# The second stage of a four-layer convolution: four x2 buffers, small products as scalar_tensor_tensor, later statistics products, and layer three's image scaled on two engines

## The reference

```python
def _gn(v, G=8, eps=1e-5):
    g = v.reshape(B_, G, C_ // G, H_, W_)
    m = jnp.mean(g, axis=(2, 3, 4), keepdims=True)
    s = jnp.var(g, axis=(2, 3, 4), keepdims=True)
    return ((g - m) / jnp.sqrt(s + eps)).reshape(v.shape)
...
    x = x + _L0_conv_ref(_gn(x), 5)          # five Newton-Schulz steps on each 128x128 plane
    x = x + _L1_conv_ref(_gn(x), L1_conv_weight_int8, L1_conv_scale_weight, L1_conv_bias)  # 8-bit input, 3x3
    x = x + _L2_conv_ref(_gn(x), L2_conv_filter_w)   # a diagonal filter of 5 taps
    x = x + _L3_conv_ref(_gn(x), L3_conv_weight)     # a 3x3 circular convolution (written with FFTs)
```

## Time and profile before

| | us |
|---|---|
| Median of three runs | 3712.34 |
| Lowest and highest of the three | 3697.12, 3731.15 |
| The profiled execution's own time | 3719.76 |
| Its span on the core | 3717.7 |

### The profile page before, as it was taken

How to read it: one execution, slowest core, us unless ns; L and a number is a source line. 1 busy time by engine, 2 the same in 40 slices (tenths; PEclk the granted TensorE clock), 3 DMA queues, 4 the chain that set the end, 5 groups by cost and what they waited for, 6 DMA issues and landing times. The chain is left out here.

```text
span 3717.7 us, 137014 instructions
## 1 busy us (share of the span) xinstructions
PE 3436.3 (92%) x58321; PEld 2903.0 (78%) x58321; DVE 2935.7 (79%) x6205; ACT 2514.6 (68%) x4686; POOL 2737.8 (74%) x3415
## 2 busy tenths in 40 slices
PE   7999999999999999999999994788888888888888
PEld 7999999999999999999999993344545455545445
DVE  5888888888888888888888885677777777777874
ACT  6766677777777767767777763676666666766763
POOL 6888888888888888888888874566666666656662
PEclk9999999999999999999999996899999999999998
DMA  2212112122211211212212212566666666666663
GB/s 67 69 58 58 61 56 68 61 60 64 69 59 58 69 58 58 69 58 58 69 58 58 69 42 73 118 159 153 144 167 145 147 166 147 165 143 144 157 145 87
DMA packets 317726, 347.23 MB, mean 93 GB/s; under 512 B 21568, under 2 KB 284224, under 8 KB 300736
## 3 DMA queue, kind: packets, MB, share of 16 engines
q1 hardware_dynamic: 317120, 338.47, 34.9%
HBM read 135.09 MB, written 134.22 MB: 72 GB/s over the span
## 5 line engine op out<-in xcount | busy, mean ns | idle before, releaser
L1462 PE MATMUL bank<-xn,wt 64*32 64x512 bf16 (+1 forms) x18432 | 969.6, 396 | 60.9 <-issue 33.8
L1462 PE MATMUL bank<-xn,wth 64*32 64x512 f16 (+1 forms) x6144 | 949.4, 396 | 9.5 <-issue 9.4
L1235 POOL TENSOR_TENSOR xn<-F,xn 128x512 f16<-128x512 f32 x512 | 539.3, 1092 | 349.1 <-ACT xn L1292 349.1
L487 ACT ACTIVATE P<-bank 128x512 f32<-128x512 f32 x1024 | 606.0, 607 | 266.0 <-PE bank L1010 155.0
L1462 PEld LDWEIGHTS bank<-xn,wt 64*32 64x32 bf16 (+1 forms) x18432 | 453.9, 95 | 201.8 <-issue 85.5
L1462 PE MATMUL bank<-xk,wt 64*32 64x512 f16 x9216 | 535.2, 384 | 66.3 <-issue 47.5
L1462 PE MATMUL bank<-xk,wth 64*32 64x512 f16 x3072 | 524.0, 384 | 17.3 <-issue 17.1
L1462 PEld LDWEIGHTS bank<-xn,wth 64*32 64x32 f16 (+1 forms) x6144 | 407.7, 95 | 151.8 <-issue 25.9
L1349 DVE SCALAR_TENSOR_TENSOR x<-bank,wu,x 128x512 f32<-128x512 f32 x512 | 367.6, 743 | 165.0 <-PE bank L1462 163.8
L1245 POOL TENSOR_TENSOR x<-x,X 128x512 f32<-128x512 f32 x256 | 322.3, 1277 | 207.8 <-ACT x L1306 207.4
L1306 ACT ACTIVATE x<-bank,bst,sws 128x512 f32<-128x512 f32 x256 | 189.3, 776 | 386.2 <-PE bank L1462 197.0
(11 more groups left out here) (147 smaller groups left out, 8501.3 us busy)
## 6 DMA issues: line engine op xcount, KB each, us to landing
xk<-xn SPq DMA_DIRECT2D x1024, 65.9 KB, 2.6
X<-in_x SPq DMA_DIRECT2D x64, 1024.0 KB, 4.8
x_scratch<-X SPq DMA_DIRECT2D x64, 1024.0 KB, 6.0
X<-x_scratch SPq DMA_DIRECT2D x64, 1024.0 KB, 6.3
out<-x SPq DMA_DIRECT2D x64, 1024.0 KB, 4.4
wf<-in_w SPq DMA_DIRECT2D x2, 192.0 KB, 6.9
wf<-in_w SPq DMA_DIRECT2D x1, 320.0 KB, 7.2
whf<-in_w1h SPq DMA_DIRECT2D x6, 1.0 KB, 5.8
```

The source lines that it names most:

```text
L487: nc.scalar.activation(into[:, 4 * q:4 * q + 4, :], banks[q][:, :].rearrange("p (m w) -> p m w", m=4), ACT.Copy).then_inc(sb, 1)
L1235: ins = nc.gpsimd.tensor_tensor(padded(xn[l][n % 2], 1)[:, a + 1:a + 5, L:L + H], F[l][:, a:a + 4, :], padded(xn[l][n % 2], 0)[:, a + 1:a ...
L1462: ins = nc.tensor.matmul(bank[cols_, :], w, v, start=(half == i == 0), stop=(half == 1 and i == length[l] - 1))
```

## The change

1. `x2` has four buffers in place of three, so the first `raise_` of an image waits for the image four before.
2. A helper `product` writes the small products of `deviations` (one) and `normalise` (three) as scalar_tensor_tensor with the scalar 1.0, in place of tensor_tensor.
3. TensorE issues `mean` after the first piece of layer three instead of before it, and `var` after the second instead of the first. VectorE takes the first `chunk_stats` of the new image ahead of `deviations`, and `normalise` after the third piece's statistics instead of the second's.
4. ScalarE issues `quotients` ahead of `root`.
5. For layer three, ScalarE writes the f16 upper half straight from `x3` (`upper3`), and VectorE writes `F3` from `x3` (`scale3`) right behind `normalise`. GpSimd's `lower(3, ...)` waits for both. Layer two keeps its two ScalarE passes.

```diff
-            THIRD = 3
-            xs = [None, x1s] + [[sb(f"x{l}_{n}", [H, NJ, H]) for n in range(k)] for l, k in ((2, THIRD), (3, THIRD))]
+            THIRD, X2 = 3, 4
+            xs = [None, x1s] + [[sb(f"x{l}_{n}", [H, NJ, H]) for n in range(k)] for l, k in ((2, X2), (3, THIRD))]
...
                         pool.wait_ge(high[l], n + 1)
+                        if l == 3:
+                            pool.wait_ge(scaled_f[3], n + 1)
...
+                    def upper3(n, b):
+
+                        act.wait_ge(scale_set, b + 1)
+                        need(act, normed[3], n)
+                        nc.scalar.activation(padded(xn[3][n % 2], 0)[:, 1:NJ + 1, L:L + H], xs_of(3, n)[:, :, :],
+                                             ACT.Identity, scale=cols["r"][:, 1:2],
+                                             bias=cols["nb"][:, 1:2]).then_inc(high[3], 1)
...
-                            need(act, evac[2], BPI * (n - 2))
+                            need(act, evac[2], BPI * (n - X2 + 1))
...
+                        if there(s + 1):
+                            quotients(s + 1)
                         if pair(s):
                             root(s - 1)
-                        if there(s + 1):
-                            quotients(s + 1)
                         if there(mid):
-                            upper(3, mid, s - 1)
+                            upper3(mid, s - 1)
...
+                    def product(out_, a, b):
+                        return nc.vector.scalar_tensor_tensor(out=out_, in0=a, scalar=1.0, in1=b, op0=ALU.mult, op1=ALU.mult)
...
-                        link.done(nc.vector.tensor_tensor(dev[:, :, :], dev[:, :, :], dev[:, :, :], ALU.mult))
+                        link.done(product(dev[:, :, :], dev[:, :, :], dev[:, :, :]))
...
+                    def scale3(n, b):
+
+                        dve.wait_ge(scale_set, b + 1)
+                        need(dve, normed[3], n)
+                        nc.vector.tensor_scalar(F[3][:, :, :], xs_of(3, n)[:, :, :], cols["m"][:, 1:2], cols["r"][:, 1:2],
+                                                ALU.subtract, ALU.mult).then_inc(scaled_f[3], 1)
...
                             whole_stats(s - 1)
-                            deviations(s - 1)
                         for u in range(BPI):
                             if there(s):
                                 chunk_stats(2, s, u)
-                            if u == 1 and pair(s):
+                            if u == 0 and pair(s):
+                                deviations(s - 1)
+                            if u == 2 and pair(s):
                                 normalise(s - 1)
+                                if there(mid):
+                                    scale3(mid, s - 1)
...
-                            mean(s - 1)
                         for u in range(BPI):
                             if there(three):
                                 piece(3, three, u)
                             if u == 0 and pair(s):
+                                mean(s - 1)
+                            if u == 1 and pair(s):
+                                if there(s):
+                                    finish(1, s, 0)
                                 var(s - 1)
```

More of the change, by code:

```diff
@@ L1387, in normalise @@
                         link.wait()
-                        link.done(nc.vector.tensor_tensor(c["rb"][:, :], c["ra"][:, :], c["ra"][:, :], ALU.mult))
+                        link.done(product(c["rb"][:, :], c["ra"][:, :], c["ra"][:, :]))
                         link.wait()
-                        link.done(nc.vector.tensor_tensor(c["rb"][:, :], c["rb"][:, :], c["ve"][:, :], ALU.mult))
+                        link.done(product(c["rb"][:, :], c["rb"][:, :], c["ve"][:, :]))
                         link.wait()
@@ L1393, in normalise @@
                         link.wait()
-                        link.done(nc.vector.tensor_tensor(c["r"][:, :], c["ra"][:, :], c["rb"][:, :], ALU.mult))
+                        link.done(product(c["r"][:, :], c["ra"][:, :], c["rb"][:, :]))
                         link.wait()
```

## The result

The changed kernel takes 3703.18 us in the median of 19 runs (3692.5 to 3717.32) against 3713.58 for the kernel before in 19 runs (3697.12 to 3731.15). The ratio is 0.9969 with a 95% interval of 0.9954 to 0.9983: 10 us faster, where I had forecast 36. The profiled execution took 3717.3 us, span 3715.1, the slowest of its runs; in this pair the traces differ by less than the medians do, so I read them for which waits moved and not for the last microseconds.

What follows compares the result with a forecast made beforehand. VectorE's chain was taken to bound the 16 short steps, which gain nothing; the 41 long ones gain 1.04 + 0.3 - 0.4 on TensorE, less 0.1. Mean 0.60 over about 60 steps gives 36 us, so 3676 us, range 3625 to 3728.

Steps and rivals of the forecast that it cites:

- `mean` one piece later: TensorE's wait for VectorE's sums at `mean`, 1.04 us a step, goes because the moved piece covers 2.1 us.
- `var`: TensorE waits at `var` for late sums of squares: +0.4 us a step, between 0 and 1.3.
- The clock: Half-clock stretches on TensorE behind `mean` go with its idle time: -0.3 us a step, between nothing and 0.43.
- Small products: On VectorE, scalar_tensor_tensor still waits for GpSimd's adds, so the exchange of operation itself is worth 0.
- The one row on which this stood: L1376 on VectorE, a scalar_tensor_tensor: median 177 ns, but 1.28 us once, at 3281.06, when an add began just before.
- Four `x2` buffers: The fourth buffer, with `quotients` ahead of `root`, gives 0; ScalarE's 174.8 us of waiting are mostly time it had to spend.
- `scale3` and the collision: VectorE's chain grows by 1.21 us for `scale3` and 1.09 for one collision of `clamp` with GpSimd's `lower(3)`.
- The upper bound of 2.2 us for `scale3`: On VectorE, `scale3` would take 2.2 us at one column per ns, as the statistics were said to have it.
- Short and long steps: 16 steps under 20 us, bound by VectorE's chain, gain nothing; 41 long ones, mean 22.1, gain 0.84 us each.
- the sign of being wrong that I had written down: Wrong if VectorE idles before `whole_stats` and steps stay at 21 us, or if products are short beside a running add.
- Layer three's upper half in one pass: ScalarE loses a 1.91 us pass; `lower(3)`, layer two and transfers into `xk` start about 1.9 earlier, without a gain term.
- an exchange of waits: Rival: all of `mean`'s wait returns at `var` and the next `mean`; within 15 us either way, 3712; chance 0.17.

Runs made afterwards that it cites:

- small store: The changed kernel with only the first of sixteen rows of each output tile stored, 64 KB an image in place of 1 MB: 3631.65 us, ratio 0.9766.

## Why the prediction was wrong

Against the forecast, point by point; per-step numbers are the totals of 2400 to 3600 us over 56 steps.

*`mean` one piece later.* Right: 1.04 forecast, 58.3 - 2.0 = 56.3 us, 1.0 a step. The kernel without `scale3`, that is the new order with the free parts alone, gained 1.6%, and the old order beside `scale3` lost some 50 us against the new one.

*`var`.* Right: 0.4 forecast, 22.0 / 56 = 0.39.

*The clock.* I took 0.3. In 2410 to 3550 us the windows of 1 us show 17 half-clock stretches before and 14 after, and 36 us lost before, 24 after, so 0.2. The size is near; the reason that I gave is wrong. I had put 14 of the stretches down to the wait at `mean` because they begin close to a `mean`. Of the 17 of before, 7 have a wait at `mean` of 1.3 to 1.9 us just ahead of them, the other 10 a stop without a releaser. With `mean`'s wait gone, 15 stretches up to 3620 us are left, more than the "fewer than ten" that I had named: 13 have such a stop (1.75 to 2.7 us) just ahead of them, two a wait for `xk` of 3.0 and 3.2 us.

*Small products.* Right at 0, and shown: exchanging the operation back changes no row. L1389, a scalar_tensor_tensor with two inputs in SBUF, turned from 177 to 1203 ns when its place came to lie beside an add. The one row on which this stood became 56. This agrees with what the Trainium skill states under "SBUF — State Buffer", "Who interferes with whom": a VectorE instruction with two inputs in SBUF contends with a GpSimd instruction that reads SBUF, with no exception for this operation.

*Four `x2` buffers.* Right at 0: 3702 with three.

*`scale3` and the collision.* 1.35 us instead of 1.21, and 0.77 us at `integers` instead of 1.09 at `clamp`: 2.12 on VectorE against 2.30 forecast. The upper bound of 2.2 us for `scale3` was misread: a statistic takes 0.69 us for 512 columns, which would make 2.8 for 2048.

*Short and long steps.* The forecast left the 16 short steps where they were and gave the long ones 0.84 us. From the first `whole_stats` after 2409 us on, 15 of 56 steps take under 20 us before, 18.98 in the mean, and the others 22.13; after, 11 take 19.67 and the others 21.68. The short ones lost 0.7 us and the long ones gained 0.45. The steps stayed at 21.27 us where I had named 20.7, and VectorE waited 2.5 us of each (69.2 us in 1200 for GpSimd's adds, 43.5 and 27.7 for TensorE). None of this lies directly ahead of `whole_stats`, but it is close to the sign of being wrong that I had written down.

*Layer three's upper half in one pass: "These had slack in most steps: no term of its own."* **This is the step that failed.** I looked at the transfers only for when ScalarE would release them, which is earlier, and not for what stands ahead of them in SyncE's queue. That is the store, released by VectorE's residuals, and the same part of the change puts 2.1 us on VectorE ahead of these and takes a pass of 1.9 us from ScalarE: the store used to leave 1.5 us ahead of the finished upper half and now leaves behind it. The transfers came later instead, by 0.6 us for the first and 1.3 for the last, and the wait for `xk` took 33.2 / 56 = 0.59 us a step. The exchange of store and transfers alone took it back (3665).

The sum with that term: 1.0 + 0.2 - 0.39 - 0.59 = 0.2 a step, 12 to 13 us over 60 steps; 10 were measured. By its number the outcome is the rival called an exchange of waits, within its 15 us, to which I gave 0.17. By its mechanism it isn't: I had the wait come back at `var` and at the next `mean`, and most of it came back at `xk`. That this rival's number came out is luck. I had also seen the price of part five as one on VectorE's chain alone (the short steps); the part alone is 40 us slower, so the change was a good order (57 us with the free parts, 3707.9 to 3650.4) and a part that ate most of it.

What stays open: why `scale3` brings TensorE's stops without a releaser from 68 to 96 us in 1100. In the kernel without it the store leaves by itself and the transfers a little later, and in the small store the stops fall with the bytes; both fit with stops that depend on what is in the queues beside the megabyte. Against it stands the kernel before with part five alone, where the transfers follow the store as closely (0.45 us) and the stops are 41.8 us. Which neighbour counts wasn't separated, nor was the loss of the kernel before with the store last. That the half-clock stretches nearly vanish in two kernels (1.00 granted) and not in the others is measured and not explained.

## What to carry to other kernels

A transfer is released by the later of two things: its own semaphore and whatever stands ahead of it in its issuing queue (here the store, 2.2 us later than the semaphore). When an edit makes one engine later, look for waits on that engine in every in-order queue, and at what is queued behind them. An edit that frees one engine by loading another can change sign with a one-line move on a third: here `scale3` cost some 50 us behind the store and gained some 35 once the store stood between the transfers.

## What the runs showed of the hardware that I had not expected

TensorE's stops without a releaser come at fixed places of its program, and mostly a few microseconds after a large transfer was issued. In 2400 to 3500 us of the kernel before, 49 of them last over 1 us. Counted in matmuls, all 48 distances from one to the next are multiples of 127.5, within one matmul. Between the first and the last of them lie 229 places so spaced. Whether TensorE stops at one depends on how long ago the later of the step's load and store was issued (stops over 0.3 us, of the places reached):

| | under 4 us ago | 4 to 7 us ago | 7 us and more |
|---|---|---|---|
| kernel before | 18 of 93 | 51 of 65 | 1 of 71 |
| changed kernel | 15 of 90 | 56 of 73 | 3 of 66 |
| changed kernel, small store | 5 of 88 | 21 of 70 | 1 of 79 |

The places in the middle column cost 1.2 us each in the mean in the kernel before, and 0.3 us with the small store.

The stops are worth 1.9 us of a 21 us step in the mean, and moving the store moves them: 100 us in 1100 with the store next to the load, 97 with it ahead of the transfers, 52 with it between them, all three on the kernel before. What a sum of them comes to depends on how many of the places meet a transfer: with part five alone on the kernel before, TensorE reached only 48 places 4 to 7 us after one and stopped at 31. What stands at these places, and what of the transfer holds TensorE there, no run shows.
